# First attention of a gated cross-attention stack: the output product placed behind the next scores, in another PSUM bank

## The chip, the cores and the metric

The kernel runs on one core of one Trainium2 chip, in one launch. The metric is the device time of that launch in microseconds (us). TensorE multiplies matrices into PSUM, VectorE and ScalarE read PSUM and work on elements, GpSimd works on SBUF alone, SyncE issues most of the DMAs. Each engine works through its own instructions in order and waits on semaphores for the others.

## The reference

Four blocks follow each other over x of 32 batches x 128 tokens x 128 channels; ctx has the same shape:

```
x = x + tanh(g_xattn[0]) * attention_0(layernorm(x), ctx)   # 16 heads of 8, biases, softmax
x = x + tanh(g_ffn[0])   * experts_0(layernorm(x))          # 8 experts over fixed slices of the tokens
x = x + tanh(g_xattn[1]) * attention_1(layernorm(x), ctx)   # 16 heads of 64
x = x + tanh(g_ffn[1])   * experts_1(layernorm(x))          # top-1 routing over 8 experts
```

The change lies in the first line. attention_0 is, for each batch, Q = xn Wq' + bq, K and V from ctx alike, softmax(Q K' / sqrt(8)) V for each of the 16 heads, and the product of the 128 concatenated head outputs with Wo. In the kernel Wo is already multiplied by tanh(g_xattn[0]), and the bias bo, multiplied too, is added to x by GpSimd beforehand, so that the last operation of a batch is x += heads Wo.

## The kernel before, in words

The first attention is the function `first_attention` (L386 on). It works batch by batch, 32 of them, as a pipeline written out by hand: `every_step` calls a function `step(n, s, live)` on each of the engines PE, DVE and ACT for n from -5 to B + 2 (B is 32); `live(k)` is true where batch n + k exists. Steps 4 to 27 are in a hardware loop of six turns of four steps each, the others are unrolled. In one step the engines work on different batches: the projection is at batch n + 3, the stacks at n + 2, the scores by query at n + 1, the scores by key at n, the sums at n - 1, the division and output at n - 2.

The parts of a batch in their order, with the lines at which the profile shows them:

- L495, L497 (DVE) take the statistics of the layernorm, GpSimd normalises (L378 to L383), PE transposes the result into the bank `front_bank` (L694), ACT and DVE split it into a high and a low half (L642, L501).
- `project` and `project_values` (L52) make Q, K and V; ACT and DVE take them out (L647, L506, L515).
- `stack_up` (L52, operands `l_qk_hi,stack_sel`) spreads Q (m = 0) and then K (m = 1) over row groups in the bank `stack_bank`, from which ACT copies each (L652). m = 1 waits until the copy of m = 0 is done.
- `score_by_query` (L735) makes the scores, two row groups at a time (unit 0 and 1), on tiles of 32 rows of TensorE, into two banks. DVE takes the negated maxima of each query from them (L520, `maxima`, four for each batch, r = 0 to 3). Unit 1 waits for the maxima r = 0 and 1, and the next batch's unit 0 for r = 2 and 3, as they free the banks.
- `transpose_maxima` (L744) transposes these maxima into columns 0 to 127 of `misc_bank`, DVE copies them (L525).
- `score_by_key` (L753, L758) makes the transposed scores with the maxima added in, also on tiles of 32 rows; ACT takes the exponentials (L656).
- `weigh` (L769) multiplies them with V and a column of ones into `sum_bank`; ACT copies that (L660), `transpose_sums` (L776) turns it back, DVE divides (L531, L533).
- `transpose_heads` (L783) transposes the 128 head outputs into columns 128 to 255 of `misc_bank`, DVE copies them (L539, `headsT`), `project_heads` (L787) multiplies them with Wo into columns 256 to 383 of `misc_bank`. This is a product of 128x128 by 128x128 in f32, and shows as two matmul instructions with two weight loads. DVE adds the result to x (L544, `add_to_x`) and counts it in the semaphore `x_done`.

In the trace `fold_bank` is the name of four PSUM banks that later serve other stages: two hold the scores, the third is `stack_bank`, the fourth `front_bank`. `l_misc` is `misc_bank`, `n_shared` holds the maxima and the heads.

PE's order in a step is: scores by query unit 0 of batch n + 1, scores by key unit 1 of n - 1, L744 of n, L776 of n - 2, values of n, stacks of Q of n + 2, projection of n + 3, scores by query unit 1 of n + 1, scores by key unit 0 of n, stacks of K of n + 2, L783 of n - 2, L769 of n - 1, L694 of n + 4, L787 of n - 2. L744 waits for `x_done` of batch n - 3, since the two share a bank and TensorE may not write to a bank that DVE reads.

DVE's order is: L501 of n + 3, L544 of n - 3, maximum 0 of n + 1, L525 of n, maximum 1, L531 and L533 of n - 2, maximum 2, L515 of n, L506 of n + 3, maximum 3, L539 of n - 2, statistics of n + 5. The last steps also take the statistics and the normalisation of the next block (L350 to L371). `load_weights` (L270), on SyncE's queue, waits once for `x_done` at 6 and then issues the first expert weights and the clearing of a buffer in HBM.

Of the kernel before, what the change touches and what calls it, by code (L numbers as in the profile page):

```python
# [13 lines left out]
ALU = mybir.AluOpType  # L14
# [7 lines left out]
P = 128  # L22
B = 32
# [362 lines left out]
def first_attention(nc, A, k):  # L386
# [16 lines left out]
    with ExitStack() as ctx:  # L403
# [37 lines left out]
        def row(t, n):  # L441
            return t[:, bass.ds(n, 1), 0:P].rearrange("p a n -> p (a n)")
# [11 lines left out]
        def there(n):  # L454
            return slice(4 * n, 4 * n + 4)

        def folded_lo(dve, n):
            dve.wait_ge(k.M_hi_ready, n + 1)
            nc.vector.scalar_tensor_tensor(out=k.M_lo[:, there(n), :], in0=k.fold_bank[n][:, :].rearrange("p (h n) -> p h n", h=4), scalar=k.tg[:, 1:2],
                                           in1=k.M_hi[:, there(n), :], op0=ALU.mult, op1=ALU.subtract).then_inc(k.M_lo_ready, 1)  # L460
# [3 lines left out]
        with nc.Block() as block:  # L464
# [10 lines left out]
            def _(dve):  # L475
# [42 lines left out]
                def maxima(n, s, r):  # L518
                    dve.wait_ge(scored, 2 * n + r // 2 + 1)
                    nc.vector.tensor_reduce(neg_max[:, s % 2, G * r:G * r + 4], a_bank[r % 2][:, :].rearrange("p (j n) -> p j n", j=4),  # L520
                                            AX.X, ALU.max, negate=True).then_inc(max_ready, 1)
# [19 lines left out]
                def add_to_x(n):  # L541
                    dve.wait_ge(projected, n + 1)
                    dve.wait_ge(bias_added, n + 1)
                    nc.vector.tensor_tensor(row(k.x_sb, n), misc_bank[:, 2 * P:3 * P], row(k.x_sb, n), ALU.add).then_inc(x_done, 1)  # L544

                def step(n, s, live):
                    if live(3):
                        transposed_lo(n + 3)
                    if live(-3):
                        add_to_x(n - 3)  # L550
                    if live(1):
                        maxima(n + 1, s + 1, 0)
                    if live(0):
                        maxima_out(n)
                    if live(1):
                        maxima(n + 1, s + 1, 1)
                    if live(-2):
                        divide(n - 2)
                    if live(1):
                        maxima(n + 1, s + 1, 2)  # L560
                    if live(0):
                        values(n, s, live(3))
                    if live(3):
                        projected_lo(n + 3, s + 3)
                    if live(1):
                        maxima(n + 1, s + 1, 3)
                    if live(-2):
                        heads_transposed(n - 2)
                    if live(5):
                        statistics(n + 5, s + 5)  # L570
                    if isinstance(n, int):
                        if n == FIRST + 1:
                            prime()
                        if n == 0:
                            k.norms.prime()
                        if n in (B - 4, B - 3):
                            dve.wait_ge(k.norms.primed, 2)
                            k.norms.statistics(dve, n - B + 4, n - B + 4, wait=False)
                        if n in (B - 2, B - 1):
                            k.norms.normalised(dve, n - B + 2, n - B + 2)  # L580
                        if n in (B - 1, B):
                            k.norms.statistics(dve, n - B + 3, (n - B + 3) % 2)
                        if n > B:
                            k.folded_lo(dve, n - B - 1)
# [102 lines left out]
            def _(pe):  # L687
# [28 lines left out]
                def stack_up(n, s, m, done):  # L716

                    if m == 1:
                        pe.wait_ge(stack_q, n + 1)
                    elif s == 0:  # L720
                        pe.wait_ge(qk_lo_ready, 2 * n + 2)
                    for j in range(4):
                        sel = [k.stack_sel[:, 2 * m + part, 4 * j:4 * j + 4].rearrange("p h c d -> p (h c d)") for part in range(2)]
                        last = both_products(nc, stack_bank[:, j * P:j * P + P], [(sel[0], qk_hi[:, s % 2, m, :]), (sel[1], qk_lo[:, s % 2, m, :])])
                    last.then_inc(done, 1)
# [13 lines left out]
                def transpose_maxima(n, s, beside):  # L739
                    if not beside:  # L740
                        pe.wait_ge(max_ready, R * n + R)
                    if s >= 3:
                        pe.wait_ge(x_done, n - 2)
                    nc.tensor.transpose(misc_bank[:, 0:P], neg_max[:, s % 2, :], k.ident[:, :]).then_inc(maxT_moved, 1)  # L744

                def score_by_key(n, s, unit):
# [37 lines left out]

                def project_heads(n):
                    pe.wait_ge(headsT_ready, n + 1)
                    nc.tensor.matmul(misc_bank[:, 2 * P:3 * P], headsT[:, :], k.wo0[:, :], start=True, stop=True).then_inc(projected, 1)  # L787

                def fold(u):
                    for t in range(4):  # L790
# [6 lines left out]
                def step(n, s, live):  # L797
                    if live(1):
                        score_by_query(n + 1, s + 1, 0)
                    if live(-1):  # L800
                        score_by_key(n - 1, s - 1, 1)
                    if live(0):
                        transpose_maxima(n, s, live(1))
                    if live(-2):
                        transpose_sums(n - 2)
                    if isinstance(n, int) and n == B:
                        pe.wait_ge(k.late_landed, 16 * 2)
                        fold(0)
                    if isinstance(n, int) and n == B + 1:
                        fold(1)  # L810
                    if live(0):
                        project_values(n, s, live(3))
                    if live(2):
                        stack_up(n + 2, s + 2, 0, q_stacked)
                    if live(3):
                        project(n + 3, live(0))
                    if live(1):
                        score_by_query(n + 1, s + 1, 1)
                    if live(0):
                        score_by_key(n, s, 0)  # L820
                    if live(2):
                        stack_up(n + 2, s + 2, 1, k_stacked)
                    if live(-2):
                        transpose_heads(n - 2, s - 2, live(0))
                    if live(-1):
                        weigh(n - 1, s - 1, live(0))
                    if live(4):
                        transpose(n + 4, s + 4)
                    if live(-2):
                        project_heads(n - 2)  # L830


                for n in range(WARM_UP):
# [1227 lines left out]
```

## Time and profile before

| what | us |
|---|---|
| median of 3 runs | 825.15 (824.63 to 825.51) |
| the profiled execution, its own time | 822.23 |
| its span from the first to the last instruction | 820.5 |
| PE busy in the span | 771.0 (94%) |
| DVE busy | 616.2 (75%) |
| ACT busy | 548.7 (67%) |
| GpSimd (POOL) busy | 469.1 (57%) |

The first attention takes the stretch from some 20 to 204 us of the span. The clock that TensorE was granted was 0.997 of full speed in the mean over the span. Matmuls are pipelined: one that is shown with 0.22 us may be followed by the next after 0.055 us, so intervals from start to start say what an instruction costs, not its duration. In a timeline, a row with xN merges N instructions that follow each other, and the bracket gives the idle time of that engine before the row and the instruction that ended it. PEld is the loading of weights into TensorE.

### The profile page before, as it was taken

How to read it: one execution, taken by the hardware profiler on the slowest of the kernel's cores; microseconds unless marked ns; L12 is line 12 of the kernel's file. 1: busy time of each engine (PE TensorE's matmuls, PEld its weight loads, DVE VectorE, ACT ScalarE, POOL GpSimd, SP SyncE). 2: the span in 40 equal slices, each digit the busy share in tenths (PEclk: the TensorE clock that was granted, in tenths of full speed). 3: DMA queues.
4: the chain of work that ended last, by engine and by line, in shares of the span. 5: the costliest groups of instructions: out<-in, count | busy, mean ns of one | idle time of the engine just before them, and what ended most of it. 6: DMA issues, size and time to landing. Idle time of an engine off the chain costs nothing. (4 is left out here: it accounts for less than half of the span.)

```text
span 820.5 us, 30377 instructions
## 1 busy us (share of the span) xinstructions
PE 771.0 (94%) x10574; PEld 632.3 (77%) x10579; DVE 616.2 (75%) x2394; ACT 548.7 (67%) x1109; POOL 469.1 (57%) x876
## 2 busy tenths in 40 slices
PE   4999999998999989999999999999999998888895
PEld 2777777776788868888888888888888886367774
DVE  5899999998777767888888887878888787434442
ACT  2687888786555568777777777777777774155652
POOL 6555777772011265767667767667767674224444
PEclk9999999999999999999999999999999999999998
DMA  8805999500200000000000000000000000122000
GB/s 230 293 2 173 276 258 242 128 1 3 71 1 0 0 2 2 3 7 7 7 7 0 7 7 7 7 7 0 7 7 7 7 7 5 41 73 63 25 29 18
DMA packets 56160, 41.69 MB, mean 51 GB/s; under 512 B 3897, under 2 KB 51651, under 8 KB 55856
## 3 DMA queue, kind: packets, MB, share of 16 engines
q1 hardware_dynamic: 52400, 36.39, 16.8%
q0 software_dynamic: 2272, 4.27, 1.6%
q10 hardware_dynamic: 1440, 0.40, 0.3%
q8 instruction: 29, 0.48, 0.2%
q14 instruction: 19, 0.16, 0.1%
HBM read 18.07 MB, written 23.44 MB: 51 GB/s over the span
## 5 line engine op out<-in xcount | busy, mean ns | idle before, releaser
L1678 PE MATMUL l_pv<-l_Z,l_probs 128*128 128x129 f32 x1024 | 164.4, 284 | 3.0 <-ACT l_probs L1506 1.4
L1678 PEld LDWEIGHTS l_pv<-l_Z,l_probs 128*128 128x128 f32 x1024 | 138.3, 191 | 21.8 <-issue 5.2
L1439 POOL TENSOR_TENSOR l_qk_lo<-w,l_qk_hi 128x512 f16<-128x512 f32 x128 | 144.5, 1159 | 0.6 <-ACT l_qk_hi L1500 0.4
L1161 DVE SCALAR_TENSOR_TENSOR x_sb<-l_pv,l_inv,x_sb 128x128 f32 (+1 forms) x256 | 89.8, 351 | 33.7 <-DVE l_inv L1148 6.5
L1496 ACT ACTIVATE w<-l_qk_bank 128x512 f32<-128x512 f32 x124 | 74.1, 597 | 53.3 <-PE l_qk_bank L52 51.6
L52 PE MATMUL l_tz<-M,cT 128*128 128x512 f16 x384 | 104.1, 380 | 0.5 <-ACT l_Z L1511 0.3
L1506 ACT ACTIVATE l_probs<-l_b 128x512 f32<-128x512 f32 x128 | 72.7, 594 | 44.4 <-PE l_b L1644 44.2
L520 DVE TENSOR_REDUCE n_shared<-fold_bank 128x4 f32<-128x512 f32 x128 | 87.4, 684 | 9.5 <-PE fold_bank L735 9.3
L1138 DVE TENSOR_REDUCE l_neg_max<-l_a 128x4 f32<-128x512 f32 x128 | 83.2, 681 | 2.2 <-PE l_a L1622 2.1
L1500 ACT ACTIVATE l_qk_hi<-w 128x512 f16<-128x512 f32 x124 | 77.4, 624 | 1.1
L1511 ACT ACTIVATE l_Z<-l_tz 128x512 f32<-128x512 f32 x124 | 74.1, 597 | 4.9 <-PE l_tz L52 1.4
L1161 DVE SCALAR_TENSOR_TENSOR l_acc<-l_pv,l_inv,l_acc 128x128 f32<-128x128 f32 x224 | 76.6, 342 | 0.0
L365 POOL TENSOR_TENSOR n_rstd<-n_var,n_half 128x4 f32<-128x4 f32 x20 | 20.2, 1009 | 87.9 <-DVE n_var L359 87.8
L1148 DVE RECIPROCAL l_inv<-l_pv 128x2 f32<-128x2 f32 x256 | 40.8, 159 | 20.1 <-PE l_pv L1678 20.1
L378 POOL TENSOR_TENSOR l_work<-l_stats,l_work 128x1 f32<-128x1 f32 x65 | 12.5, 192 | 72.8 <-DVE l_stats L497 44.0
L1405 POOL TENSOR_TENSOR l_taker<-l_taker 128x1 f32<-128x1 f32 x95 | 17.7, 193 | 62.8 <-DVE l_slot_i L1234 24.8
L52 PE MATMUL l_qk_bank<-cT,w_hi 128*128 (+1 forms) x504 | 52.5, 219 | 0.0
L52 PEld LDWEIGHTS l_tz<-M,cT 128*128 (+1 forms) x384 | 33.3, 98 | 20.1 <-ACT l_Z L1511 0.4
L652 ACT ACTIVATE l_stack<-fold_bank 128x512 f16<-128x512 f32 x64 | 39.0, 610 | 13.1 <-PE fold_bank L52 13.1
L1880 POOL DMA_INDIRECT out<-f_result,f_token x39 | 38.6, 989 | 13.8 <-issue 11.1
L52 PE MATMUL l_qk_bank<-l_T_hi,w_hi 128*128 128x128 f16 x252 | 45.8, 220 | 0.0
L52 PE MATMUL l_qk_bank<-cT,w_lo 128*128 (+1 forms) x252 | 45.5, 219 | 0.0
(291 smaller groups left out, 2287.6 us busy)
## 6 DMA issues: line engine op xcount, KB each, us to landing
expert_rows<-empty_row SPq DMA_DIRECT2D x8, 2178.0 KB, 23.6
x_sb<-expert_rows SPq DMA_DIRECT2D x36, 66.0 KB, 2.4
x_sb<-in_x SPq DMA_DIRECT2D x4, 512.0 KB, 6.5
ctx_sb<-in_ctx SPq DMA_DIRECT2D x4, 512.0 KB, 7.7
w<-in_L_ffn_w SPq DMA_DIRECT2D x1, 2048.0 KB, 9.2
w_raw<-in_L_ffn_gate_w SPq DMA_DIRECT2D x1, 1408.0 KB, 9.9
w_raw<-in_L_ffn_up_w SPq DMA_DIRECT2D x1, 1408.0 KB, 12.0
downT<-in_L_ffn_down_w SPq DMA_DIRECT2D x2, 512.0 KB, 4.0
```

The source lines that it names most:

```text
L52: last = nc.tensor.matmul(out, lhsT, rhs, start=start and n == 0, stop=stop and n == len(pairs) - 1, skip_group_check=True)
L520: nc.vector.tensor_reduce(neg_max[:, s % 2, G * r:G * r + 4], a_bank[r % 2][:, :].rearrange("p (j n) -> p j n", j=4), AX.X, ALU.max, negat ...
L652: nc.scalar.activation(stack[:, s % DEEP, m].rearrange("p j n -> p (j n)"), stack_bank[:, :], ACT.Copy).then_inc(ready, 1)
L1138: nc.vector.tensor_reduce(neg_max[:, at:at + Q], a_bank[half][:, :].rearrange("p (t n) -> p t n", t=Q), AX.X, ALU.max, negate=True).then_i ...
L1148: nc.vector.reciprocal(inv[:, 2 * m:2 * m + 2], O[:, :, P]).then_inc(inv_ready, 1)
L1161: nc.vector.scalar_tensor_tensor(out=total, in0=O[:, h, 0:P], scalar=inv[:, j:j + 1], in1=total, op0=ALU.mult, op1=ALU.add).then_inc(summe ...
L1439: nc.gpsimd.tensor_tensor(qk_lo[:, w, m, Q * u:Q * u + Q].rearrange("p t n -> p (t n)"), qk[:, u, m, :], qk_hi[:, w, m, Q * u:Q * u + Q].r ...
L1496: nc.scalar.activation(qk[:, u, m, :], qk_bank[:, :], ACT.Copy).then_inc(qk_ready, 1)
L1500: nc.scalar.activation(qk_hi[:, w, m, Q * u:Q * u + Q].rearrange("p t n -> p (t n)"), qk[:, u, m, :], ACT.Copy)\
L1506: nc.scalar.activation(probs[:, at:at + Q, :].rearrange("p h n -> p (h n)"), b_bank[half][:, :], ACT.Exp, scale=float(HD1) ** -0.5).then_i ...
L1511: nc.scalar.activation(Z[:, w, Q * q:Q * q + Q, 0:P], tz_bank[:, :].rearrange("p (h n) -> p h n", h=Q), ACT.Copy)\
L1678: last = nc.tensor.matmul(pv_bank[m % 2][:, h * (P + 1):(h + 1) * (P + 1)], probs[:, 2 * m + h, :], Z[:, w, 2 * m + h, :], start=True, sto ...
```

## The change

`project_heads` is called in the next step, for batch n - 3, behind the scores by query unit 0 and the scores by key unit 1, and ahead of `transpose_maxima`. It writes to columns 256 to 383 of `stack_bank`, apart from the last two batches, for which it stays with `misc_bank`. The wait for `x_done` goes from `transpose_maxima` to the stacks of Q (`stack_up` with m = 0), where batch n + 2 waits until x of batch n - 3 is done. On DVE the first maximum of a step goes ahead of L501 and L544. No instruction is added or taken away but waits.

```diff
+        def projected_bank(n):
+            return misc_bank if isinstance(n, int) and n >= B - 2 else stack_bank
...
                 def add_to_x(n):
                     dve.wait_ge(projected, n + 1)
                     dve.wait_ge(bias_added, n + 1)
-                    nc.vector.tensor_tensor(row(k.x_sb, n), misc_bank[:, 2 * P:3 * P], row(k.x_sb, n), ALU.add).then_inc(x_done, 1)
+                    nc.vector.tensor_tensor(row(k.x_sb, n), projected_bank(n)[:, 2 * P:3 * P], row(k.x_sb, n), ALU.add).then_inc(x_done, 1)
 
                 def step(n, s, live):
+                    if live(1):
+                        maxima(n + 1, s + 1, 0)
                     if live(3):
                         transposed_lo(n + 3)
                     if live(-3):
                         add_to_x(n - 3)
-                    if live(1):
-                        maxima(n + 1, s + 1, 0)
                     if live(0):
                         maxima_out(n)
...
                     elif s == 0:
                         pe.wait_ge(qk_lo_ready, 2 * n + 2)
+                    if m == 0 and s >= 5:
+                        pe.wait_ge(x_done, n - 4)
                     for j in range(4):
...
                 def transpose_maxima(n, s, beside):
                     if not beside:
                         pe.wait_ge(max_ready, R * n + R)
-                    if s >= 3:
-                        pe.wait_ge(x_done, n - 2)
...
                 def project_heads(n):
                     pe.wait_ge(headsT_ready, n + 1)
-                    nc.tensor.matmul(misc_bank[:, 2 * P:3 * P], headsT[:, :], k.wo0[:, :], start=True, stop=True).then_inc(projected, 1)
+                    nc.tensor.matmul(projected_bank(n)[:, 2 * P:3 * P], headsT[:, :], k.wo0[:, :], start=True, stop=True).then_inc(projected, 1)
...
                     if live(-1):
                         score_by_key(n - 1, s - 1, 1)
+                    if live(-3):
+                        project_heads(n - 3)
                     if live(0):
                         transpose_maxima(n, s, live(1))
...
                     if live(4):
                         transpose(n + 4, s + 4)
-                    if live(-2):
-                        project_heads(n - 2)
```

## Rows read from the trace of the kernel before

**Rows 1.** Tile view of `l_misc`: engine, op, count: durations ns min/median/max, first and last start.

```profile
L787 PE MATMUL l_misc<-wo,n_shared x64: 275/326/377, 41.1 to 203.7; 128*128 128x128 f32 x64
...
L744 PE MATMUL l_misc<-ident,n_shared x32: 303/328/474, 26.4 to 193.6; 128*128 128x128 f32 x32
```

**Rows 2.** Waits, 35 to 205 us: who waited for whom, us in total, times, longest.

```profile
PEld l_misc L787 <- DVE n_shared L539: 9.5, 30, 0.6
...
PEld l_misc L744 <- DVE x_sb L544: 1.7, 8, 0.3
```

**Rows 3.** Timeline of PE in one step, to L787 of the next: start, length, instruction.

```profile
122.49 0.33 PE L694 MATMUL fold_bank<-ident,n_shared 128*128 128x128 f32 x1
122.93 0.49 PE L787 MATMUL l_misc<-wo,n_shared 128*128 128x128 f32 x2
123.35 0.23 PE L735 MATMUL fold_bank<-l_stack 32*128 32x128 f16 x2
...
123.97 0.33 PE L744 MATMUL l_misc<-ident,n_shared 128*128 128x128 f32 x1
124.13 0.60 PE L776 MATMUL l_sum_bank<-ident,downT 128*128 128x128 f32 x4
124.57 0.22 PE L52 MATMUL fold_bank<-w0T_hi,cT 128*128 128x128 f16 x1
...
124.74 0.22 PE L52 MATMUL fold_bank<-l_qk_hi,stack_sel 128*128 128x128 f16 x1
...
125.61 0.23 PE L735 MATMUL fold_bank<-l_stack 32*128 32x128 f16 x2
...
128.31 0.49 PE L787 MATMUL l_misc<-wo,n_shared 128*128 128x128 f32 x2
```

**Rows 4.** Timeline of DVE in the same step.

```profile
121.99 0.68 DVE L520 TENSOR_REDUCE n_shared<-fold_bank 128x4 f32<-128x512 f32 x1
122.59 0.28 DVE L539 COPY n_shared<-l_misc 128x128 f32<-128x128 f32 x1
...
123.18 0.17 DVE L497 BATCH_NORM_AGGREGATE l_stats<-l_bn 128x2 f32<-128x6 f32 x1
123.42 0.29 DVE L501 TENSOR_TENSOR l_T_lo<-fold_bank,l_T_hi 128x128 f16<-128x128 f32 x1
123.63 0.28 DVE L544 TENSOR_TENSOR x_sb<-l_misc,x_sb 128x128 f32 x1
123.83 0.68 DVE L520 TENSOR_REDUCE n_shared<-fold_bank 128x4 f32<-128x512 f32 x1
...
126.05 0.69 DVE L520 TENSOR_REDUCE n_shared<-fold_bank 128x4 f32<-128x512 f32 x1 [0.26 <-PE fold_bank L735]
```

**Rows 5.** Timeline at the end of step 1, which has no output product.

```profile
35.22 0.68 DVE L520 TENSOR_REDUCE n_shared<-fold_bank 128x4 f32<-128x512 f32 x1
...
35.69 0.33 PE L694 MATMUL fold_bank<-ident,n_shared 128*128 128x128 f32 x1
...
36.05 0.23 PE L735 MATMUL fold_bank<-l_stack 32*128 32x128 f16 x2
```

**Rows 6.** Timeline of PE in the second attention.

```profile
400.05 0.61 PE L1678 MATMUL l_pv<-l_Z,l_probs 128*128 128x129 f32 x4
```

**Rows 7.** Timeline of DVE at a turn of the loop.

```profile
112.55 0.29 DVE L501 TENSOR_TENSOR l_T_lo<-fold_bank,l_T_hi 128x128 f16<-128x128 f32 x1 [0.26 <-ACT l_T_hi L642]
112.86 0.29 DVE L544 TENSOR_TENSOR x_sb<-l_misc,x_sb 128x128 f32 x1
```

**Rows 8.** Timeline of PEld and PE at the same turn.

```profile
112.44 0.33 PE L735 MATMUL fold_bank<-l_stack 32*128 32x128 f16 x5
...
113.20 0.14 PEld L744 LDWEIGHTS l_misc<-ident,n_shared 128*128 128x128 f32 x1 [0.20 <-DVE x_sb L544]
```

**Rows 9.** Timeline of PE in the last steps.

```profile
190.06 0.34 PE L735 MATMUL fold_bank<-l_stack 32*128 32x128 f16 x5 [0.47 <-DVE n_shared L520]
...
193.56 0.30 PE L744 MATMUL l_misc<-ident,n_shared 128*128 128x128 f32 x1 [0.28 <-DVE x_sb L544]
```

## The prediction

> **What bounds the kernel now.** The page and the times first: the profiled execution spans 820.5 us and took 822.23 with what lies around it; the median of the three runs shown is 825.15, that is 2.92 above it. I work out a difference against the profiled execution and take it off the median. The change touches the first attention alone. Its place is read from the tile view of the bank misc: TensorE transposes the maxima (L744) 32 times from 26.4 to 193.6 us [rows 1], 31 intervals of 5.39 us in the mean. An attention step is worth 5.4 us, and 0.1 us in each is 3 us of the whole. The later stages hold nothing that the change touches, so what is saved here moves them forward as they are.
>
> Second view: who waited for whom in this stretch. The one wait of TensorE that comes in nearly every step is that of the output product L787 for the vector engine's copy of the transposed heads, L539: 9.5 us in 30 waits [rows 2], 0.32 us each. Eight waits of L744 for the addition to x (L544) come to 1.7 us [rows 2].
>
> Third view: one step in order of time. TensorE starts L694 at 122.49, stands still, starts L787 at 122.93, the scores L735 at 123.35, L744 at 123.97, L776 at 124.13, the value product at 124.57, the stacks at 124.74 and the second scores L735 at 125.61 [rows 3]. VectorE's third maximum of a batch starts at 126.05, 0.44 behind those scores, after 0.26 of idle time; its fourth starts at 121.99 and ends at 122.67, then comes the copy L539 until 122.87 [rows 4], and 0.06 later L787 starts [rows 3]. From L787 to the next L787 it is 5.38 us (128.31 - 122.93) [rows 3]. The loop that sets it runs scores, third and fourth maximum, copy, output product, scores. Both engines are nearly full: VectorE's slack in a step is that 0.26 and little more.
>
> **What is removed: L787 with its wait between L694 and the next scores.** Today L694 to L735 is 123.35 - 122.49 = 0.86 us [rows 3]. The nearest row for it without L787 is step 1, which has no output product yet: L694 at 35.69, L735 at 36.05, 0.36 [rows 5]. The scores start 0.50 earlier. The lower bound of that gap is the wait that stays, for the fourth maximum: 122.67 + 0.06 = 122.73, 0.24 behind L694 [rows 4]. I take 0.36, because it is measured between the same two instructions. That row cannot say whether VectorE or TensorE itself held L735: its fourth maximum starts at 35.22 and at 0.68 us ends at 35.90 [rows 5]. The Trainium skill, in "TensorEngine Tiling (Array Packing)", Key Properties, says that changing the tiling mode drains TensorE; L735 works on tiles of 32 rows, L694 on the whole array. By that rule the gap could not fall under L694's 0.33 us, and the gain would stay near my value; without it the gap would be 0.24 and the gain 0.12 more per step. The rule speaks against the larger gain.
>
> **What is added: L787 between the scores by key (L758) and L744.** Its two instructions span 0.49 us [rows 3] and the shortest one takes 0.275 [rows 1], so the second starts 0.215 behind the first. In a stream such an instruction takes 0.11: four of L1678, nearly the same form, span 0.61 [rows 6], and less the 0.275 of one that leaves three intervals of 0.11. L744, now second, starts 0.215 + 0.11 = 0.325 later; and L744 to L776, 0.16 now [rows 3], falls to 0.11, since L787 has paid for the restart. Added: 0.325 - 0.05 = 0.275. Bounds: 0.42, what L787 takes today from its start to the next one's (123.35 - 122.93) [rows 3], and 0.22, two in a stream. Net per step: 0.50 - 0.275 = **0.225**, between 0.50 - 0.42 = 0.08 and 0.62 - 0.22 = 0.40. The upper end is cut by the loop through VectorE: third maximum to end of the fourth 2.00 us (126.05 less a period of 5.38, to 122.67), 0.06, first to second scores 125.61 - 123.35 + 0.275 = 2.535, 0.44 [rows 3, 4]: 5.04 us, a gain of at most 0.34.
>
> **What is moved on VectorE, and the new wait.** The first maximum goes ahead of L501 and L544; the queue has the same work. Shift the step by the numbers above: L735 at 122.85, L787 at 123.47 (the copy has ended at 122.87, its wait is gone), L744 at 123.80, L776 at 123.91, values at 124.35, stacks at 124.52, second scores at 125.39. The first maximum needs the scores: 122.85 + 0.44 = 123.29; VectorE's L497 starts at 123.18 and today L501 follows at 123.42 [rows 4]. I put it at 123.35. Then L501 at 123.95 (0.60 as from 123.83 on), L544 at 124.16, 0.21 behind as today [rows 4], ended at 124.44, seen by TensorE at 124.50. The new wait sits before the stacks, at 124.52: a dead heat, with 0.05 us at most lost if the maximum starts at 123.42. Queued behind it are the stacks, the projection and the second scores, for which ScalarE and VectorE wait. The value product also needs L501's result: 123.95 + 0.29 + 0.06 = 124.30 against 124.35, free. The second maximum starts at 124.57 and ends at 125.25, ahead of the second scores at 125.39. The later output of L544 disturbs nothing else: ScalarE's copy of the stacks and the scores behind it have their waits before and after alike. The DMA queue's wait for six finished batches and POOL's work only move with x. Taking L744's old wait away costs nothing.
>
> At the turns of the hardware loop, every fourth step, VectorE's L501 comes after 0.26 us of idle time and L544 0.31 behind it [rows 7], and the load of L744 waits 0.20 for L544 [rows 8]. With the first maximum at 112.55, L501 is at 113.15, L544 at 113.46, seen at 113.80; the stacks would be ready at 112.44 - 0.50 + 1.67 = 113.61 (L735 of [rows 8], and 1.67 from 122.85 to 124.52). The 0.20 moves from L744 to the stacks: such steps win the same 0.225.
>
> At the end, steps 29 and 30 are VectorE's: L735 waits 0.47 for the second maximum [rows 9]; I count nothing there. In step 31 the 0.28 of L744's matmul on L544 goes [rows 9]; with what follows I estimate 0.4 in all.
>
> **Sum.** Steps 2 to 28 are 27: 27 x 0.225 = 6.1, and 0.4: **6.5 us**. 822.23 becomes 815.7, 825.15 becomes 818.7.
>
> **Rivals.**
> (a) Small gain: L787 keeps its 0.42, or the new wait costs 0.05 to 0.15 in every step. Speaking for it: the dead heat above; against it, L1678's 0.11. 27 x 0.08 = 2.2: 823.0.
> (b) Large gain: L694 to L735 shrinks to 0.24 and VectorE sets the pace at about 0.33 per step: 27 x 0.33 + 0.4 = 9.3: 815.8. For it: step 1's L735 may have been VectorE's. Against: VectorE's slack of 0.26 [rows 4], which such a step would use up. The rule of the Trainium skill on the drain, above, is against it too.
> (c) The change removes nothing: the 0.30 stands again, at the stacks, because the addition to x now sits behind a maximum of 0.60. It needs L544 0.2 later than my dead heat; nothing in the rows gives that [rows 4]: 825.15.
> (d) Slower: what the loop's turn costs VectorE, 0.26 + 0.10 [rows 7], stands in every step ahead of the addition (waiting for the scores, then for L787, now one behind the other). It decides once L544's end reaches TensorE more than 0.225 behind the stacks' own time; at 0.36 each step loses 0.36 - 0.02 - 0.225 = 0.12, 27 x 0.12 = 3.2: 828.4. Against it: the scores are there at 123.29, before VectorE is free.
>
> **How the numbers follow.** Forecast 0.66, (a) 0.12, (b) 0.11, (c) 0.05, (d) 0.06. A measurement of this kernel tells some 0.2%, 1.65 us, from no change. Forecast and (b) are faster; (a) at 2.2 is so mostly: 0.09 of its 0.12. Faster 0.86, same 0.08, slower 0.06. The range runs from (b), 815.8, lowered to 815.4 for the scatter of the runs, to (a), 823.0. (c) and (d) stay outside.
>
> **What would show it.** Right: the wait of L787 for L539 is gone from the list, L694 to L735 is about 0.36, L758's end to L776 0.275 longer, L744 from step to step 5.15 us, VectorE's idle time before the third maximum about 0.1, and a wait of the stacks for L544 of 0.2 at the loop's turns alone. Wrong: a wait for L544 in every step (a, c, d by its size), L787 taking 0.42 again, or L735 waiting for the fourth maximum right behind L694 (b). An attention that gains what I say with a whole that does not would break the claim that the later stages only shift.

## The result, and the profile after

| | before | changed |
|---|---|---|
| median of 5 runs, us | 824.63 (823.04 to 825.51) | 818.23 (817.28 to 820.78) |
| profiled execution, its own time | 822.23 | 818.23 |
| its span | 820.5 | 816.5 |

The ratio is 0.9928, with a 95% interval of 0.9912 to 0.9945: 6.4 us by the medians, 4.5 to 7.3 by the interval. In a second set of runs, in which the kernel before takes 812.91, the changed one takes 807.19: 0.9929 (0.9909 to 0.9949).

In the changed kernel the lines have moved down by 3 (L740 for the scores by 5): L520 is now L523, L544 L547, L539 L542, L501 L504, L694 L697, L735 L740, L744 L747, L776 L779, L787 L790. The waits of TensorE from 25 to 205 us, us in total, times, longest:

```profile
PEld fold_bank L697 <- issue: 6.4, 29, 0.7
...
PEld fold_bank L52 <- issue: 2.6, 7, 0.5
...
PEld fold_bank L740 <- ACT l_stack L655: 2.3, 7, 0.5
PE fold_bank L52 <- DVE l_T_lo L504: 2.2, 7, 0.6
...
PEld fold_bank L52 <- DVE l_T_lo L504: 1.8, 3, 0.9
...
PEld l_misc L790 <- DVE n_shared L542: 0.6, 1, 0.6
...
PEld fold_bank L52 <- DVE x_sb L547: 0.5, 1, 0.5
```

The 30 waits of the output product [rows 2] are down to one, in the unrolled end. No wait for another engine stands in every step any more. What is new is a wait of the value product (L52) for VectorE's L504 at seven places: five turns of the loop and the first two steps. The waits for ScalarE's copy of the stacks (L655), 7 instead of 3, all lie in the first and last steps. The timeline of PE in an ordinary step:

```profile
124.86 0.33 PE L697 MATMUL fold_bank<-ident,n_shared 128*128 128x128 f32 x1
125.12 0.28 PE L740 MATMUL fold_bank<-l_stack 32*128 32x128 f16 x4
...
125.76 0.49 PE L790 MATMUL fold_bank<-wo,n_shared 128*128 128x128 f32 x2
126.09 0.27 PE L747 MATMUL l_misc<-ident,n_shared 128*128 128x128 f32 x1
126.20 0.60 PE L779 MATMUL l_sum_bank<-ident,downT 128*128 128x128 f32 x4
126.63 0.22 PE L52 MATMUL fold_bank<-w0T_hi,cT 128*128 128x128 f16 x1
...
126.80 0.22 PE L52 MATMUL fold_bank<-l_qk_hi,stack_sel 128*128 128x128 f16 x1
...
127.68 0.23 PE L740 MATMUL fold_bank<-l_stack 32*128 32x128 f16 x2
...
129.94 0.33 PE L697 MATMUL fold_bank<-ident,n_shared 128*128 128x128 f32 x1
```

From L697 to L697 it is 5.08 us (5.38 before); the ordinary steps take 5.08 to 5.10, 5.09 in the text from here on. L697 to the scores takes 0.26 us where it was 0.86 with the output product and its wait [rows 3]; L790 to L747 takes 0.33, L747 to L779 0.11. VectorE in the same step:

```profile
124.36 0.68 DVE L523 TENSOR_REDUCE n_shared<-fold_bank 128x4 f32<-128x512 f32 x1
124.96 0.28 DVE L542 COPY n_shared<-l_misc 128x128 f32<-128x128 f32 x1
...
125.64 0.66 DVE L523 TENSOR_REDUCE n_shared<-fold_bank 128x4 f32<-128x512 f32 x1
126.22 0.28 DVE L504 TENSOR_TENSOR l_T_lo<-fold_bank,l_T_hi 128x128 f16<-128x128 f32 x1
126.41 0.28 DVE L547 TENSOR_TENSOR x_sb<-fold_bank,x_sb 128x128 f32 x1
126.61 0.28 DVE L528 CAST l_neg_maxT<-l_misc 128x128 bf16<-128x128 f32 x1
```

The copied heads are there at 125.24 and the product starts at 125.76: half a microsecond of cover. The addition ends at 126.69, the stacks that wait for it start at 126.80. At a turn of the loop the branch comes ahead of the first maximum on DVE, and the value product on PE waits for L504:

```profile
131.07 0.69 DVE L523 TENSOR_REDUCE n_shared<-fold_bank 128x4 f32<-128x512 f32 x1 [0.28 <-issue]
131.68 0.28 DVE L504 TENSOR_TENSOR l_T_lo<-fold_bank,l_T_hi 128x128 f16<-128x128 f32 x1
131.88 0.28 DVE L547 TENSOR_TENSOR x_sb<-fold_bank,x_sb 128x128 f32 x1
```

```profile
132.10 0.23 PE L52 MATMUL fold_bank<-w0T_hi,cT 128*128 128x128 f16 x1 [0.22 <-DVE l_T_lo L504]
```

Such a step takes 5.48 us (5.68 before). To compare kernels apart from the start of the program, which differs by some us from one execution to the next, I take the 24 steps from the transposed maxima of batch 4 to those of batch 28. Before they run from 47.70 to 178.35, 130.65 us; after, by the timeline of PE:

```profile
48.28 0.27 PE L747 MATMUL l_misc<-ident,n_shared 128*128 128x128 f32 x1
...
172.66 0.27 PE L747 MATMUL l_misc<-ident,n_shared 128*128 128x128 f32 x1
```

124.38 us, 6.27 less. The two profiled spans differ by 4.0 only. What is missing was lost in three places.

**The start.** The maxima of batch 0 are transposed at 26.47 (26.43 before), those of batch 4 at 48.28 (47.70): 0.54 more for four steps that should have gained. PE in the first step, before and, below it, after:

```profile
26.43 0.47 PE L744 MATMUL l_misc<-ident,n_shared 128*128 128x128 f32 x1
26.70 0.31 PE L52 MATMUL fold_bank<-w0T_hi,cT 128*128 128x128 f16 x1
26.81 0.31 PE L52 MATMUL fold_bank<-w0T_lo,cT 128*128 128x128 f16 x1
```

```profile
26.47 0.47 PE L747 MATMUL l_misc<-ident,n_shared 128*128 128x128 f32 x1
27.53 0.29 PE L52 MATMUL fold_bank<-w0T_hi,cT 128*128 128x128 f16 x1 [0.58 <-DVE l_T_lo L504]
27.61 0.31 PE L52 MATMUL fold_bank<-w0T_lo,cT 128*128 128x128 f16 x1
```

From the transposed maxima to the value product it is 1.06 us instead of 0.27, and in the second step 0.80 (32.83 to 33.63) instead of 0.16 (32.04 to 32.20). L504 now stands behind the first maximum, which waits for the scores, and in these steps there is no output product ahead of L747 and there are no sums behind it to cover that. From the value product to the next maxima the first step takes 5.30 us, 5.34 before, so the loss of that step is this wait. The first two steps lose 1.18, the next two gain 0.64. With VectorE's old order (run e1 below) the value product follows 0.24 and 0.17 behind the maxima, without a wait.

**The second attention.** From the last addition to x (204.0 before, 197.7 after) to its first scores (299.2 and 294.3) another 1.4 is lost. That is the clock. The windows of the changed kernel (busy time of PE, PEld, DVE, ACT, POOL, then the granted clock, DMA share, GB/s):

```profile
24.00:28.00 4.00, 2.84 (x23) 1.85 (x22) 3.65 (x11) 0.94 (x3) 1.50 (x5) 0.50 1.03 433
...
288.00:292.00 4.00, 4.00 (x31) 2.38 (x29) 1.94 (x19) 2.13 (x6) 3.69 (x11) 0.67 0.02 4
```

Around 290 us it ran for a while at the lower level, 1.2 GHz, and the rows agree: the first products L52 there take 0.31 us (287.29), 0.22 before (293.60), where the profile shows 1.00; the expert block ahead of that takes the same 87.2 us in both (203.47 to the last L987 at 290.67, and 197.13 to 284.33). The start is different. There too the windows show 0.50 after and 1.00 before, but the rows above say otherwise: in both kernels the products L52 take 0.31 us and start some 0.11 apart, twice what they do later (0.22 and 0.055), so both ran at the lower level. The pace rises at some 29.7 us before and 31.1 after.

**The end.** 1.2 is lost from the last weighted values (697.4, 692.2) to the end, whose clock is alike within 0.01 and for which I have no cause. The five runs of the changed kernel have mean clocks of 0.985 to 0.991; runs of the kernel before, taken beside the experiments, spread from 0.984 to 0.997. The profile of the kernel before, at 0.997, is at the upper end of that, and its 822.23 lies under all five of its timed runs, so the medians are the fairer comparison.

### The profile page after: what moved, and what is told of

The parts are those of the page before. It is cut to its first block and busy times, and to the rows that moved or that the text cites. A ratio compares the mean times of both kernels' runs of the same rounds, so it can differ in the third digit from the quotient of the medians.

```text
span 816.5 us, 30376 instructions
## 1 busy us (share of the span) xinstructions
PE 766.9 (94%) x10574; PEld 632.4 (77%) x10579; DVE 613.5 (75%) x2394; ACT 548.5 (67%) x1109; POOL 469.2 (57%) x876
## 5 line engine op out<-in xcount | busy, mean ns | idle before, releaser
L52 PE MATMUL l_tz<-M,cT 128*128 128x512 f16 x384 | 104.8, 382 | 0.5 <-ACT l_Z L1514 0.2
L523 DVE TENSOR_REDUCE n_shared<-fold_bank 128x4 f32<-128x512 f32 x128 | 87.1, 680 | 10.4 <-PE fold_bank L740 7.5
L655 ACT ACTIVATE l_stack<-fold_bank 128x512 f16<-128x512 f32 x64 | 39.1, 610 | 22.8 <-PE fold_bank L52 22.8
L52 PE MATMUL l_qk_bank<-cT,w_hi 128*128 (+1 forms) x504 | 53.1, 220 | 0.0
L52 PEld LDWEIGHTS l_tz<-M,cT 128*128 (+1 forms) x384 | 33.5, 98 | 20.3 <-ACT l_Z L1514 0.4
L52 PE MATMUL l_qk_bank<-cT,w_lo 128*128 (+1 forms) x252 | 46.0, 220 | 0.0
L52 PE MATMUL l_qk_bank<-l_T_hi,w_hi 128*128 128x128 f16 x252 | 45.8, 220 | 0.0
```

The source lines that it names most:

```text
L52: last = nc.tensor.matmul(out, lhsT, rhs, start=start and n == 0, stop=stop and n == len(pairs) - 1, skip_group_check=True)
```

## The experiments

Each gives its 24 steps, measured as above, beside the whole, which moves by up to 5 us between runs of one kernel (810.3 to 815.6 for the kernel before in one set). The runs were made in sets: beside e1 to e4 the kernel before takes 823.25, beside the others 812.9 to 813.3, so a run is compared with the kernel before of its own set.

**One part at a time.** The changed kernel with VectorE's old order:

```diff
                 def step(n, s, live):
-                    if live(1):
-                        maxima(n + 1, s + 1, 0)
                     if live(3):
                         transposed_lo(n + 3)
                     if live(-3):
                         add_to_x(n - 3)
+                    if live(1):
+                        maxima(n + 1, s + 1, 0)
```

> The changed kernel with the vector engine's old order (L501 split of the transpose, addition to x, then the first maximum). Theory (the three parts belong together): the addition now waits for the output product, which ends 0.64 + 0.49 = 1.13 us behind the start of the first scores, so addition at +1.16, first maximum at +1.36 instead of +0.52, second maximum about +2.2 and the second scores 0.3 to 0.35 later per step than in the changed kernel: step 5.4 us instead of 5.09, the whole within 2 us of the kernel before (some 825). Rival (the vector engine's order is incidental, TensorE's saved wait is all): step 5.1, whole some 818.

Measured: 826.09 against 823.25, ratio 1.0047 (1.0029 to 1.0064). Steps of 5.55 us, the 24 take 133.59, 9.2 more than changed and 2.9 more than before. DVE and, below it, PE:

```profile
113.65 0.29 DVE L547 TENSOR_TENSOR x_sb<-fold_bank,x_sb 128x128 f32 x1 [0.18 <-PE fold_bank L790]
113.86 0.68 DVE L523 TENSOR_REDUCE n_shared<-fold_bank 128x4 f32<-128x512 f32 x1
```

```profile
112.41 0.23 PE L740 MATMUL fold_bank<-l_stack 32*128 32x128 f16 x2
...
115.39 0.28 PE L740 MATMUL fold_bank<-l_stack 32*128 32x128 f16 x4 [0.41 <-DVE n_shared L523]
```

The addition starts 1.24 behind the scores, the first maximum 1.45 (1.16 and 1.36 expected), and TensorE waits for the second. The mechanism is the expected one and costs 0.46 a step instead of 0.3 to 0.35; the whole ends 2.8 above the kernel before where at most 2 was expected. The order on VectorE is no detail: without it the change loses.

The bank alone, with the product at its old place:

```diff
                 def project_heads(n):
                     pe.wait_ge(headsT_ready, n + 1)
+                    if projected_bank(n) is stack_bank and not (isinstance(n, int) and n + 4 >= B):
+                        pe.wait_ge(stack_k, n + 5)
...
-                    if live(-3):
-                        project_heads(n - 3)
...
+                    if live(-2):
+                        project_heads(n - 2)
```

(and VectorE's old order). In its old place the product now also has to wait until the stacks of K have left the bank (`stack_k`).

> The kernel before with one part: the output product stays at the end of the step but goes to the bank of the stacks, and the wait for x done goes from the transposed maxima to the stacks. Theory: the 0.30 us wait for the copied heads stays in each step, only the wait of the transposed maxima (2.0 us in all) goes and returns in part at the loop's turns: 0.5 to 1.5 us faster than before. Rival (the bank is what brought the gain, because the transposed maxima no longer depend on the addition): 5 to 6 us faster.

Measured: 823.57, ratio 1.0007 (0.9992 to 1.0021). 24 steps 129.51, 1.1 less than before, which the whole cannot tell. By its list of waits the old one stands, and the rival falls:

```profile
PEld fold_bank L792 <- DVE n_shared L542: 8.6, 28, 0.6
```

The order alone, and the move alone, in the kernel before:

```diff
+                    if live(1):
+                        maxima(n + 1, s + 1, 0)
                     if live(3):
                         transposed_lo(n + 3)
                     if live(-3):
                         add_to_x(n - 3)
-                    if live(1):
-                        maxima(n + 1, s + 1, 0)
```

> The kernel before with the vector engine's new order alone: first maximum, then L501 and the addition. The transposed maxima still wait for the addition. Theory: first maximum at 0.48 us behind the first scores, L501 at 1.08, addition at 1.29, done and seen at 1.63, so L744 starts at 1.65 instead of 0.62, about 1.0 us of standstill in a step less the 0.3 of slack elsewhere: 20 to 30 us slower. Rival (TensorE's wait is absorbed by the other engines' slack): under 5 us slower.

Measured: 854.54, 1.0382 (1.0352 to 1.0412), 31 us slower, a little beyond the 20 to 30 expected; steps of 6.34, 24 take 152.90. A load of weights of L744 stands for 1.11:

```profile
116.71 0.14 PEld L744 LDWEIGHTS l_misc<-ident,n_shared 128*128 128x128 f32 x1 [1.11 <-DVE x_sb L544]
```

```diff
+                    if live(-3):
+                        project_heads(n - 3)
                     if live(0):
                         transpose_maxima(n, s, live(1))
...
-                    if live(-2):
-                        project_heads(n - 2)
```

> The kernel before with the output product behind the next scores, but in the old bank, old order on the vector engine, transposed maxima waiting for the addition as before. Theory: L744 now waits for output product, addition and two semaphores in a row, 0.49 + 0.03 + 0.28 + 0.06 = 0.86 us instead of 0.33, and the first maximum comes after the addition, 0.8 us late; against that the 0.30 wait and the gap before the scores are gone: 0.4 to 0.8 us longer steps, 10 to 22 us slower. Rival (moving the product is the gain): 5 us faster.

Measured: 832.94, 1.0120 (1.0091 to 1.0148), 9.7 us slower, at the lower end of what was expected; steps of 5.79, 24 take 139.02:

```profile
106.39 0.14 PEld L744 LDWEIGHTS l_misc<-ident,n_shared 128*128 128x128 f32 x1 [0.68 <-DVE x_sb L544]
```

So per ordinary step: bank -0.04, move +0.41, order +0.96, bank and move without the order +0.17, all three -0.30. The bank frees the transposed maxima from the addition, the move covers the product's wait, the order takes the addition out of the way of the maxima; no part gains what the three do. Of the pairs only bank and move was run. The order with the bank alone, and the order with the move alone, were not, so that each of these two parts is needed beside the order is argued and not shown.

**What sets 5.09 us now.** VectorE's work between the third and the fourth maximum made lighter (the values of 14 of 16 heads are not written):

```diff
-                    nc.vector.tensor_tensor(V[:, s % 2, :, 0:D0], front_bank[:, P:2 * P].rearrange("p (h d) -> p h d", h=H),
-                                            k.bv0[:, :].rearrange("p (h d) -> p h d", h=H), ALU.add).then_inc(V_ready, 1)
+                    nc.vector.tensor_tensor(V[:, s % 2, 0:2, 0:D0], front_bank[:, P:P + 2 * D0].rearrange("p (h d) -> p h d", h=2),
+                                            k.bv0[:, 0:2 * D0].rearrange("p (h d) -> p h d", h=2), ALU.add).then_inc(V_ready, 1)
```

> The changed kernel with the vector engine's addition of the bias of V (L518, between the third and the fourth maximum) done for 2 of 16 heads, so that the values of the others are not written; the fourth maximum ends about 0.1 us earlier. Theory D (TensorE's own change to tiles of 32 rows sets the 0.26 us from L697 to the scores, by the end of L697): that gap and the step of 5.09 us stay. Theory V (the wait for the fourth maximum sets it): the gap falls to 0.16 and the step to 5.0 us, 2 to 3 us in all.

Measured: 804.92 against 813.32, 0.9915 (0.9897 to 0.9932). DVE's fourth maximum and PEld's loads:

```profile
77.56 0.68 DVE L523 TENSOR_REDUCE n_shared<-fold_bank 128x4 f32<-128x512 f32 x1
```

```profile
78.17 0.14 PEld L697 LDWEIGHTS fold_bank<-ident,n_shared 128*128 128x128 f32 x1 [0.20 <-issue]
78.43 0.17 PEld L740 LDWEIGHTS fold_bank<-l_stack 32*128 32x128 f16 x5
```

The maximum ends at 78.24, 0.19 ahead of the load, where it was 0.08 (125.04 to 125.12), and the gap stays 0.26 in every step from 50 to 120 us. The load waits for ScalarE's copy of the stacks too, which ends 0.16 ahead of it in both kernels. Run e1 settles that one:

```profile
111.55 0.60 ACT L655 ACTIVATE l_stack<-fold_bank 128x512 f16<-128x512 f32 x1
...
112.15 0.14 PEld L697 LDWEIGHTS fold_bank<-ident,n_shared 128*128 128x128 f32 x1 [0.20 <-issue]
...
112.41 0.11 PEld L740 LDWEIGHTS fold_bank<-l_stack 32*128 32x128 f16 x4
```

The copy ends at 112.15, 0.26 ahead of the load, the fourth maximum 0.16 ahead, and the gap is 0.26 again. The scores wait for nothing but these two here, so TensorE itself makes the gap. The ordinary step is 5.05 to 5.08, and the 24 take 123.10, 1.6 less than in e5: the turns are shorter (5.37 for 5.48) and the rest is spread. By the whole alone, 2.3 us under the changed kernel's 807.19 in the other set, the theory of the fourth maximum could not have been told from this one; the gap tells them apart. The other direction, one more copy ahead of the fourth maximum:

```diff
+                    if live(1) and live(0):
+                        nc.vector.tensor_copy(spare[:, 0:32], k.bv0[:, 0:32])
                     if live(1):
                         maxima(n + 1, s + 1, 3)
```

> The changed kernel with one added copy of 32 columns on the vector engine just ahead of the fourth maximum, about 0.1 us. By both theories the fourth maximum, which ends 0.07 us before the weights of the scores load, becomes the later one: the gap from L697 grows by 0.07 to 0.1 and the step too, 2 to 3 us in all. Rival (the vector engine has 0.16 us of slack in a step and takes it): no difference.

Measured: 811.77, 0.9980 (0.9963 to 0.9996), some 4.6 us above the changed kernel's 807.19; 24 steps 128.10, 3.4 more than in e5. The maximum ends at 80.03:

```profile
80.08 0.17 PEld L743 LDWEIGHTS fold_bank<-l_stack 32*128 32x128 f16 x6 [0.19 <-DVE n_shared L524]
```

The gap from L700 at 79.75 is 0.33 and the step 5.18, 0.09 more, as expected: VectorE's idle time elsewhere in the step is of no help. I had not expected its turns: in four of them 5.98 to 5.99 instead of 5.48, where the same load waits 0.59 for the same maximum. The trace shows why: in these four turns the added copy itself takes 0.58 us, in all other steps 0.17.

```profile
95.19 0.58 DVE L570 COPY l_spare<-bv 128x32 f32<-128x32 f32 x1
...
100.78 0.17 DVE L570 COPY l_spare<-bv 128x32 f32<-128x32 f32 x1
```

So the turns say nothing of what a small delay costs there. The output product doubled in place:

```diff
+                    nc.tensor.matmul(projected_bank(n)[:, 2 * P:3 * P], headsT[:, :], k.wo0[:, :], start=True, stop=True)
                     nc.tensor.matmul(projected_bank(n)[:, 2 * P:3 * P], headsT[:, :], k.wo0[:, :], start=True, stop=True).then_inc(projected, 1)
```

> The changed kernel with the output product done twice in its new place (same operands, same output). Theory (TensorE's stream sets the step, and this product costs 0.11 us for each instruction behind the first): 0.22 us per step, 32 steps, 6 to 7 us. Rival (it lies in slack): under 2 us.

Measured: 811.03, 0.9977 (0.9957 to 0.9998), 3.8 us above the changed kernel. L790 to L747 takes 0.55 (104.95 to 105.50) instead of 0.33, the step 5.30 instead of 5.09: 0.11 for each instruction, and all of it in the step. The 24 steps take 128.28, 3.5 more than in e5. That is less than the 6 to 7 expected, because the steps with a turn hardly grow (5.47 to 5.54, from 5.48): there the product lies in the wait.

**The turn of the loop.** The changed kernel in the same set of runs as the next two:

> The changed kernel unaltered, on the same chip as the two below, to tell them from it: 6 to 7 us under the kernel before.

Measured: 807.19 against 812.91; 24 steps 124.74. The loop with 8 and with 12 steps in a turn:

```diff
-            with engine.Fori(*LOOP) as i:
-                for s in range(DEEP):
-                    step(DEEP * i + s, DEEP * LOOP[0] + s, lambda ahead: True)
+            with engine.Fori(1, 4) as i:
+                for s in range(2 * DEEP):
+                    step(2 * DEEP * i + (s - DEEP), DEEP * LOOP[0] + s, lambda ahead: True)
```

> The changed kernel with 8 steps in a turn of the hardware loop and 3 turns instead of 6. A step with a turn takes 5.48 us in the changed kernel and 5.09 without. Theory (the turn costs the vector engine its branch, and TensorE waits for it at the values and stacks): three turns fewer save 3 x 0.39 = 1.2 us against the changed kernel. Rival (the cost is in fetching instructions, and stays with the number of instructions): no difference, or a loss from the longer body.

> The same with 12 steps in a turn and 2 turns. Theory: 4 x 0.39 = 1.6 us faster than the changed kernel, steps of 5.48 us at two places only. Rival: no difference or slower.

Measured: 840.46, 1.0336 (1.0311 to 1.0362), and 837.47, 1.0302 (1.0268 to 1.0336); the 24 steps take 160.56 and 151.86. Both theories are missed by far; the rival, a loss from the longer body, had the direction and named no size. With 8 steps, batches 9 to 20 have steps of up to 15.27 us; PE stands at the scores for nothing that the profile shows:

```profile
105.94 0.40 PE L740 MATMUL fold_bank<-l_stack 32*128 32x128 f16 x4 [6.81 <-issue]
```

The page's queue for instructions, in the changed kernel and then in the loop of 8:

```profile
q8 instruction: 29, 0.48, 0.2%
```

```profile
q8 instruction: 51, 0.84, 0.4%
```

22 more packets of instructions. Meanwhile the clearing of the expert rows, 8 transfers of 2.2 MB, fills the DMA engines. (The granted clock falls too, to 0.70 from 100 to 130 us, behind the standstills, so a part of the loss may be the clock's.) So I moved it to the first expert block:

```diff
                 k.ffn0_total = load_weights(nc, sp, A, k, x_done)
-                for e in range(E):
-                    sp.dma_start(k.expert_rows[e * REGION:(e + 1) * REGION, :].rearrange("(j p) w -> p j w", p=P),
...
                     sp.dma_start(k.downT[0:rows, c, :, :].rearrange("p e n -> p (e n)"), A["L1_ffn_down_w"][c0:c0 + rows, :]).then_inc(k.down_landed, 16)
+                for e in range(E):
+                    sp.dma_start(k.expert_rows[e * REGION:(e + 1) * REGION, :].rearrange("(j p) w -> p j w", p=P),
...
```

> The loop of 8 steps again, with the clearing of the expert rows (8 transfers of 2.2 MB) issued in the first expert block instead of during the first attention. Theory (the longer body has its instructions fetched anew in every turn, and the fetches queue behind the clearing): with the DMA queues empty the steps of 6 to 15 us go, most of the 33 us comes back, and the whole ends within 10 us of the changed kernel. Rival (a body of this length stalls by itself): still 20 us or more above it.

Measured: 820.28, 1.0089 (1.0059 to 1.0119). The 24 steps take 139.48 (160.56 in the loop of 8, 124.74 in the changed kernel), and standstills are shorter:

```profile
99.83 0.22 PEld L737 LDWEIGHTS fold_bank<-l_stack 32*128 32x128 f16 x7 [3.72 <-issue]
```

Of 36 us, 21 go with the clearing and 15 stay; the whole ends 13 above the changed kernel, between the two expectations. The meeting with the transfers makes the larger part, and the longer body costs something without them. The packets of instructions do not go with the clearing: from 60 to 170 us the queue has 1 in the changed kernel, 17 in the loop of 8 and 20 here. That what TensorE stands for is the fetching itself is argued from these packets, not shown. Last, the branch put where VectorE is idle:

```diff
-                def step(n, s, live):
+                def first_half(n, s, live):
                     if live(1):
                         maxima(n + 1, s + 1, 0)
...
                     if live(-2):
                         divide(n - 2)
+
+                def second_half(n, s, live):
                     if live(1):
                         maxima(n + 1, s + 1, 2)
...
-                every_step(dve, step)
+                def rotated(n, s, live):
+                    second_half(n, s, live)
+                    first_half(n + 1, s + 1, lambda ahead: live(ahead + 1))
+
+                every_step(dve, rotated)
```

> The changed kernel with the vector engine's loop body starting at the third maximum instead of the first: same instructions in the same order, only the branch of the hardware loop falls where the vector engine has its 0.16 us of idle time, and no longer ahead of the first maximum and the addition that TensorE waits for. Theory: steps with a turn fall from 5.48 to some 5.2 us, the others stay at 5.09, 6 x 0.28 = 1.7 us less than the changed kernel (0.2%); the waits of TensorE for L504 and L547 at the turns go. Rival (the turn's cost is TensorE's own branch): 5.48 stays.

Measured: 804.53 against 813.33, 0.9902 (0.9869 to 0.9935), the fastest that was run. By the whole it cannot be told from the changed kernel, since the intervals overlap; by the steps it can. Those at a turn take 5.15 to 5.21, and the waits for L504 at the turns are gone; in their place the load of the scores waits 0.17 to 0.22 there for the fourth maximum. The 24 take 122.76 us by the timeline of PE (L753 is L747 there),

```profile
49.06 0.27 PE L753 MATMUL l_misc<-ident,n_shared 128*128 128x128 f32 x1
...
171.82 0.27 PE L753 MATMUL l_misc<-ident,n_shared 128*128 128x128 f32 x1
```

2.0 less than the changed kernel in e5, where 1.7 was expected. The rival, TensorE's own branch, falls.

## Why the prediction was right, point by point

The forecast was 6.5 us and 818.7; measured are 6.4 and 818.23. The mechanism is the one given: the product's wait is gone and the loop is shorter by it, and e1 to e4 show that no part of the change gets there alone. The sizes of its terms agree less well than the sum, and that the sum agrees to 0.1 us is luck. In the first attention 6.3 us were gained (last addition to x at 197.7 for 204.0): 0.9 more than forecast in the 24 steps, 1.0 less in the four steps ahead of them. And between the two profiled executions the whole gained 4.0 only; the 6.4 is that of the medians.

- **Removed.** 0.50 per step was taken, for a gap of 0.36 from L694 to the scores, after [rows 5]. Measured are 0.26, so 0.60 was removed. This term was mis-sized: step 1 is a poor stand-in, its row says nothing of what held the scores, as I had written, and I took it all the same. The bound of 0.24 was nearly the value.
- **The drain.** With e8 and e1 the gap keeps its 0.26 when the fourth maximum and the copy of the stacks are early, so it is TensorE that holds the scores. The Trainium skill, "TensorEngine Tiling (Array Packing)", Key Properties, says that a change of the tiling mode drains it; the trace agrees so far as the gap is 0.26 us here and 0.11 between the f32 instructions L747 and L779, which are in one mode. No run sets the change of mode apart from all else. My reading that the gap could therefore not fall under L694's 0.33 does not hold: the next weights load at 125.12, 0.07 ahead of L697's end at 125.19, which the profile models and does not measure.
- **Added.** 0.275 was taken; from L740 to L790 it is 0.64 (0.62 before, to L744), then 0.33 and 0.11: 0.02 + 0.33 - 0.05 = 0.30. L1678's 0.11 carried over, and e10 measures it in place.
- **Net.** 0.225 was forecast, 0.30 came, inside the bounds of 0.08 and 0.34. Over 24 steps, five of them with a turn, 6.27 came instead of 5.4.
- **The start.** Steps 0 and 1 were put at nothing, without a reason, and steps 2 and 3 at 0.45 together. Measured are a loss of 1.18 and a gain of 0.64. The order on VectorE that keeps the maxima early makes the value product wait for L504 where nothing else fills TensorE; the prediction had set these two against each other for the ordinary step alone.
- **The new wait.** The dead heat fell on the right side: addition seen at about 126.75, stacks at 126.80, no wait in an ordinary step. Rivals (c) and (d), which needed one, fall with that.
- **The turns.** 0.225 was forecast, 0.20 came, but by another wait than named. I had checked L504 against the value product for the ordinary step (124.30 against 124.35) and not for the turn, where the branch makes it late too; it, not the addition, holds TensorE first.
- **The end.** From batch 28's maxima to the last addition 25.65 us became 25.04: 0.6, and 0.6 was forecast (0.4, and 0.225 for step 28).
- **Rivals.** (b) was nearer in the size of the step than my forecast (0.33). Its cause is not quite wrong either: scores to second scores 2.56, to the third maximum 0.44, to the end of the fourth 2.00 and 0.08 to the load make 5.08, so the loop through VectorE, which I had put at 5.04, comes out as long as the step within the 0.02 to which the wait can be read (after e9 the load could have followed at 0.05). e8 shows that TensorE holds the step without it (the maximum 0.11 earlier, the step some 0.03 shorter, the gap unchanged), e9 that 0.09 more on VectorE is paid in full. (a) falls: L790 to L747 is 0.33 and not 0.42, and in e10 each further instruction costs 0.11.

That the later stages only shift was claimed too simply. They do so but for the 1.4 us that the lower clock took at the start of the second attention in this execution, and for the 1.2 at the end, whose cause stays open.

## What to carry to other kernels

A wait in a stream that is nearly full on two engines is best removed by putting work of the same engine between producer and consumer; but then follow every resource that the moved instruction shares, a bank and a queue order here: the product moved alone made the step 0.41 us longer, the order changed alone 0.96. Follow them through the first steps of the pipeline as well, where less work lies between: two steps lost 1.18 us here. Where the trace has no row for the new neighbours, the bounds are worth more than a row from the ramp of the pipeline: here the bound was 0.24, the ramp's row 0.36 and the value 0.26. And a loop's branch costs what waits behind it: cut the body where the engine has its slack, rather than making the body longer.

## What the runs showed of the hardware that was not expected

- A hardware loop of 8 or 12 such steps is 30 to 33 us slower than one of 4, by standstills of up to 7.6 us, with 21 or 22 more packets on the instruction queue; with 8 steps, 21 of the 36 us in the 24 steps go when large transfers are kept out of that time.
- The same copy of 32 columns on VectorE takes 0.17 us in 27 steps of e9 and 0.58 in four that hold a turn of the loop; these steps are 5.98 us instead of 5.48. The cause of the long copies stays open.
- The granted clock of a window can mislead: from 20 to 29 us the profile of the kernel before shows 1.00 while its f16 products start 0.11 us apart, as at the lower level, and not 0.055. The spacing of equal instructions is the surer sign.
- The changed kernel starts its steps at different times: the maxima of batch 4 are transposed at 48.28 us in one profile and at 51.38 in another, while the 24 steps after it repeat within 0.4 us (124.38 and 124.74). Small changes are better read from the steps than from the whole.
